# A one-core transformer block: a separate place for one running sum, and the next batch's tokens and keys prepared earlier

## What is computed

```python
def _tc_rmsnorm(x, t, gw, gb, bw, bb):
    g = (t @ gw.T + gb)[:, None, :]
    b = (t @ bw.T + bb)[:, None, :]
    return g * x * rsqrt(mean(x * x, -1) + EPS) + b

x1 = x + attention(_tc_rmsnorm(x, t, g1w, g1b, b1w, b1b), Wq, Wk, Wv, Wo)
y  = x1 + swiglu(_tc_rmsnorm(x1, t, g2w, g2b, b2w, b2b), gate_w, hid_w, out_w)
return x + y
```

## Time and profile before

| | before |
|---|---|
| median of 3 runs | 2479.52 us |
| lowest, highest | 2472.38, 2492.58 us |
| the profiled execution, device time | 2483.76 us |
| its span, first to last instruction | 2481.9 us |
| PE busy | 2309.7 us (93%) |
| DVE busy | 1676.2 us (68%) |
| POOL busy | 1454.4 us (59%) |
| ACT busy | 1310.9 us (53%) |
| mean granted TensorE clock | 0.976 |

### The profile page before, as it was taken

How to read it: one execution, slowest core, us unless ns; L and a number is a source line. 1 busy time by engine, 2 the same in 40 slices (tenths; PEclk the granted TensorE clock), 3 DMA queues, 4 the chain that set the end, 5 groups by cost and what they waited for, 6 DMA issues and landing times. The chain is left out here.

```text
span 2481.9 us, 40287 instructions
## 1 busy us (share of the span) xinstructions
PE 2309.7 (93%) x10884; PEld 1572.9 (63%) x10884; DVE 1676.2 (68%) x2732; ACT 1310.9 (53%) x2319; POOL 1454.4 (59%) x1351
## 2 busy tenths in 40 slices
PE   5999989999989999989999848999999999999999
PEld 4655436554447555456554336888888888888887
DVE  4776734667725776537777347887788778778877
ACT  3366762566752667734667724445444534454454
POOL 0388981689970888944889925731572166216711
PEclk8999999999989999999999978999999999999999
DMA  5212203212122122132222043115412541254125
GB/s 179 81 41 63 64 14 108 52 41 67 48 71 64 38 69 52 47 95 52 51 57 60 21 162 136 60 60 179 151 54 69 170 154 52 74 164 157 47 81 174
DMA packets 92656, 209.60 MB, mean 84 GB/s; under 512 B 15632, under 2 KB 15632, under 8 KB 90640
## 3 DMA queue, kind: packets, MB, share of 16 engines
q1 hardware_dynamic: 91344, 202.71, 27.2%
q0 software_dynamic: 1088, 4.19, 0.4%
HBM read 134.23 MB, written 19.92 MB: 62 GB/s over the span
## 5 line engine op out<-in xcount | busy, mean ns | idle before, releaser
L680 DVE TENSOR_REDUCE pmax<-bank 128x1 f32<-128x512 f32 x1024 | 653.7, 684 | 197.0 <-PE bank L893 187.6
L599 ACT ACTIVATE probs<-bank 128x512 f32<-128x512 f32 x1024 | 572.0, 600 | 330.6 <-PE bank L973 249.5
L447 POOL TENSOR_TENSOR sums<-sums,probs 128x512 f32<-128x512 f32 x512 | 641.4, 1291 | 0.5 <-ACT probs L599 0.5
L447 POOL TENSOR_TENSOR sums<-probs 128x512 f32<-128x512 f32 x256 | 320.4, 1282 | 380.6 <-ACT probs L599 258.9
L973 PE MATMUL bank<-qs,ks 128*128 128x512 f32 x1024 | 441.3, 439 | 40.0 <-ACT probs L599 37.9
L893 PE MATMUL bank<-ks,qs 96*128 96x512 f32 x1024 | 402.9, 406 | 25.8 <-DVE pmax L680 25.1
L973 PEld LDWEIGHTS bank<-qs,ks 128*128 128x128 f32 x1024 | 192.8, 191 | 323.4 <-ACT probs L599 167.3
L1536 PE MATMUL bank<-H_hi,wt_hi 128*128 128x512 f32 x896 | 350.0, 391 | 14.6 <-DVE H_lo L1391 14.6
L1550 PE MATMUL bank<-ow,aw 128*128 128x512 f32 x1536 | 358.7, 392 | 0.0
L1536 PE MATMUL bank<-H_lo,wt_hi 128*128 128x512 f32 x896 | 349.6, 390 | 0.0
L1536 PE MATMUL bank<-H_hi,wt_lo 128*128 128x512 f32 x896 | 349.5, 390 | 0.0
(11 more groups left out here) (139 smaller groups left out, 3233.8 us busy)
## 6 DMA issues: line engine op xcount, KB each, us to landing
raw<-in_gu_w SPq DMA_DIRECT2D x66, 512.0 KB, 3.6
wo_raw<-in_out_w SPq DMA_DIRECT2D x128, 256.0 KB, 2.6
ks<-qk_hi SPq DMA_DIRECT2D x136, 128.0 KB, 2.4
qs<-qk_hi SPq DMA_DIRECT2D x264, 64.0 KB, 2.0
x<-in_x SPq DMA_DIRECT2D x10, 1024.0 KB, 5.2
ks<-qk_lo SPq DMA_DIRECT2D x68, 128.0 KB, 2.4
qs<-qk_lo SPq DMA_DIRECT2D x132, 64.0 KB, 2.0
wv<-wv_parts SPq DMA_DIRECT2D x4, 2048.0 KB, 8.9
```

What stands on the lines that cost most here:

```text
L447: nc.gpsimd.tensor_tensor(sums[:, h, :], first, probs[:, s % 2, h, :], ALU.add) \
L599: nc.scalar.activation(probs[:, s % 2, h, :], sbank[i % SB][:], ACT.Exp, scale=SCALE).then_inc(st_done, 1)
L680: nc.vector.reduce_max(pmax[:, t, h, hf:hf + 1], mbank[n % MB][:], AX_X).then_inc(sq_done, 1)
```

## The change

- The sum of head 0 in quad 0 goes into `yout[:, 0, :]`, a tile that the units do not otherwise use, and D of quad 0 reads it from there. POOL's wait for PE's reading of the previous quad moves from head 0 to head 1, in both quads. In unit 0 POOL waits instead for the store from `yout`.
- ACT's squares for the next batch no longer write their unused output to `yout` but to a half of `qk_hi`, after the copies of an earlier K have been stacked.
- Tokens of the next batch: half 0 is loaded in unit 1 instead of 3. Squares move from (u, s) = (4, 4) to (3, 4) and from (6, 3) to (5, 5), mean squares from (4, 5) and (6, 5) to (3, 5) and (5, 7), inverse roots on POOL from (4, 5) and (6, 6) to (3, 6) and (6, 0), scaling from (4, 6) and (6, 7) to (4, 1) and (6, 2).
- DVE's waits for the next batch's gain and bias move from (5, 0) to (4, 2), and so does ACT's.
- Transposed tokens: half 0 from unit 5 (cells 9, 13, 17, 24) to unit 4 (cells 15, 18, 24) and unit 5 (cell 8); half 1 from unit 7 (cells 13, 16, 19, 23) to unit 6 (cells 14, 17, 24) and unit 7 (cell 0). `load_x` of half 1 waits for the last tile of half 0, as before.
- The Q projections of the even units take four cells in a row instead of every second one. ("K", 8, 1) moves from cells 26 to 29 of unit 7 to cells 13 to 16.

```diff
-PROJECTED = {("K", 2, 1): (0, 1), ("Q", 2): (9, 2)}
+PROJECTED = {("K", 2, 1): (0, 1), ("Q", 2): (9, 1)}
 for odd in (1, 3):
     PROJECTED.update({("Q", odd + 2): (odd * UNIT, 1), ("K", odd + 3, 0): (odd * UNIT + 14, 1),
-                      ("K", odd + 3, 1): ((odd + 1) * UNIT, 1), ("Q", odd + 3): ((odd + 1) * UNIT + 9, 2)})
-PROJECTED.update({("Q", NU - 1): (5 * UNIT, 1), ("Q", NU): (6 * UNIT + 8, 2), ("K", NU, 0): (7 * UNIT + 8, 1),
-                  ("K", NU, 1): (7 * UNIT + 26, 1)})
-HT_AT = {5: (9, 13, 17, 24), 7: (13, 16, 19, 23)}
+                      ("K", odd + 3, 1): ((odd + 1) * UNIT, 1), ("Q", odd + 3): ((odd + 1) * UNIT + 9, 1)})
+PROJECTED.update({("Q", NU - 1): (5 * UNIT, 1), ("Q", NU): (6 * UNIT + 8, 1), ("K", NU, 0): (7 * UNIT + 8, 1),
+                  ("K", NU, 1): (7 * UNIT + 13, 1)})
+HT_AT = {(4, 15): (0, 0), (4, 18): (1, 0), (4, 24): (2, 0), (5, 8): (3, 0),
+         (6, 14): (0, 1), (6, 17): (1, 1), (6, 24): (2, 1), (7, 0): (3, 1)}
...
+    def sum_place(quad, h):
+        return yout[:, 0, :] if (quad, h) == (0, 0) else sums[:, h, :]
...
-                    if u == 3:
+                    if u == 1:
                         load_x(b, 0, prepared)
...
-                        if (u, s) == (4, 5):
+                        if (u, s) == (3, 6):
                             inverse_root(b, b * 2 + 2)
-                        if (u, s) == (6, 6):
+                        if (u, s) == (6, 0):
                             inverse_root(b, b * 2 + 3)
...
                             pool.wait_ge(st_done, SCORES_T(b, NT + n * GH + h + 1) + SB)
-                            if s % QT == 1 and h == 0:
+                            if (u, s, h) == (0, 1, 0):
+                                pool.wait_ge(y_stored[0], b * (NT // 2 * 16) + 16)
+                            if s % QT == 1 and h == 1:
                                 pool.wait_ge(w_ready, MISC(b, sums_before(u, s // QT)))
...
-                            first = probs[:, 0, h, :] if s % QT == 1 else sums[:, h, :]
-                            nc.gpsimd.tensor_tensor(sums[:, h, :], first, probs[:, s % 2, h, :], ALU.add) \
+                            total = sum_place(s // QT, h)
+                            first = probs[:, 0, h, :] if s % QT == 1 else total
+                            nc.gpsimd.tensor_tensor(total, first, probs[:, s % 2, h, :], ALU.add) \
...
-                    if b is not None and hf == 0:
-                        for s in y_stored:
-                            act.wait_ge(s, b * (NT // 2 * 16) + 16)
+                    if b is not None:
+                        for s in k_stacked:
+                            act.wait_ge(s, b * (NG * HEAD_INC) + (3 + hf) * HEAD_INC)
...
-                nc.scalar.activation(yout[:, 0, :], x_tokens(b, hf)[:, t, :], ACT.Square,
+                unused = yout[:, 0, :] if b is None else qk[0][:, 1, :].bitcast(F32)
+                nc.scalar.activation(unused, x_tokens(b, hf)[:, t, :], ACT.Square,
...
-                            if (u, s) == (4, 4):
+                            if (u, s) == (3, 4):
                                 square(b, 0, h)
-                            if (u, s) == (4, 6):
+                            if (u, s) == (4, 1):
                                 scale_x(b, 0, h)
-                            if (u, s) == (6, 3):
+                            if (u, s) == (5, 5):
                                 square(b, 1, h)
-                            if (u, s) == (6, 7):
+                            if (u, s) == (6, 2):
                                 scale_x(b, 1, h)
...
-                        if (u, s) == (4, 5):
+                        if (u, s) == (3, 5):
                             mean_square(b, 0)
-                        if (u, s) == (6, 5):
+                        if (u, s) == (5, 7):
                             mean_square(b, 1)
...
-                    last = nc.tensor.matmul(wbank[DH * h:DH * h + DH, :], ones[:], sums[:, h, :], start=True, stop=True)
+                    last = nc.tensor.matmul(wbank[DH * h:DH * h + DH, :], ones[:], sum_place(quad, h), start=True, stop=True)
```

More of the change, by code:

```diff
@@ L105, in made_at @@
     q = s * GH + h
-    if u in HT_AT and q in HT_AT[u]:
-        return ("hT", HT_AT[u].index(q), list(HT_AT).index(u))
+    if (u, q) in HT_AT:
+        return ("hT", *HT_AT[u, q])
     return ("mT", u + 1) if (s, h) == MAXIMA_AT and u < NU - 1 else None
@@ L585, in _ @@
                         act.wait_ge(pv_done, b * (NU * NS) + n + 1)
-                        if u == 5 and s == 0:
+                        if u == 4 and s == 2:
                             act.wait_ge(const_dve, b * 2 + 4)
@@ L779, in _ @@
                                                     ALU.max).then_inc(const_dve, 1)
-                        if (u, s) == (4, 5):
+                        if (u, s) == (3, 5):
                             mean_square(b, 0)
-                        if (u, s) == (6, 5):
+                        if (u, s) == (5, 7):
                             mean_square(b, 1)
-                        if (u, s) == (5, 0):
+                        if (u, s) == (4, 2):
                             dve.wait_ge(const_dve, b * 2 + 4)
```

## The result

| | before | after |
|---|---|---|
| median, us | 2479.98 (5 runs) | 2501.84 (5 runs) |
| lowest, highest | 2472.38, 2492.58 | 2499.19, 2504.41 |
| span of the profiled execution | 2481.9 | 2502.6 |
| DVE busy | 1676.2 | 1757.1 |

The ratio of after to before is 1.009, with a 95% interval of 1.0071 to 1.0108. The forecast was 2444 us, its range 2425 to 2472: wrong in size and in sign.

The account below looks back on a forecast made before the run. POOL's loop was taken to bound plain units, 1.3 us above PE's, and POOL to set unit 7's end. Terms summed to −10.1 us per batch, put at −9.0, four times −36: 2444 us, range 2425 to 2472.

Parts of the forecast that it names:

- What bounds the kernel, and the place: Plain units: POOL's loop, 34.9 us, exceeds PE's 33.55; with the place PE sets the length, gaining 4.0 up to unit 4.
- The moved work: Token tiles moved between units 4 to 7: unit 4 +1.7 us, unit 6 +2.1, unit 5 −1.8 to 33.3.
- The Q projections: Four cells in a row make DVE wait for ACT's copy: 0.5 us each in units 0 and 2, bound 1.2.
- Unit 7 and the tail: POOL ends 37.7 us into unit 7; unit and tail take 59.0 us against 68.3, a gain of 9.3.
- The step that failed: Moved work in other units: claimed none conflicts on the shared port, as tokens' low parts read PSUM and one SBUF tile.
- the rule about the shared port: DVE operations with two SBUF inputs and GpSimd operations reading SBUF exclude each other; used for 0.9 us in unit 7.
- Half of it: Rival: DVE bounds units 4 and 6, 2.5 us more in each, −16 us in all: 2464; chance 0.18.
- Slower by the clock: Rival: idle time in units 5 and 7 holds the tail's matmuls at 1.2 GHz, +60 us, 2540; chance 0.08.

Follow-up runs that it names:

- experiment 1: The kernel before with only the place for head 0 and the squares' unused output in `qk_hi`; tokens, K and Q unmoved: 2440.79 us, ratio 0.9852.
- experiment 3: The kernel after with the next batch's mean squares on ACT instead of DVE, at (3, 5) and (5, 6): 2458.41 us, ratio 0.9913.
- experiment 4: The kernel of experiment 3, with POOL also waiting in unit 7 for DVE's first two low parts of the output: 2436.40 us, ratio 0.9826.
- experiment 9: The kernel of experiment 4 with the Q projections of units 0 and 2 at every second cell again: 2429.95 us, ratio 0.9791.
- experiment 6: The kernel after with POOL's inverse roots four additions earlier, at (3, 5) and (5, 7): 2467.74 us in one run.
- experiment 7: The kernel of experiment 4 with a needless DVE tensor_scalar of 128 x 4 in five places of each batch: 2473.85 us in one run.
- experiment 10: The kernel after with POOL's two pauses for the low parts of the output, mean squares still on DVE: 2490.13 us in one run.
- experiment 11: The kernel after with POOL's wait at head 0 again in the second quad only: 2456.0 us in one run.
- experiment 2: The kernel after without the place for head 0, so the moves alone; POOL waits for D at head 0 again: 2462.11 us, ratio 0.9929.
- experiment 5: The kernel after with both POOL waits back at head 0, the sum still in `yout`: 2465.55 us in one run.

## Why the prediction was wrong

**What bounds the kernel, and the place: right in kind.** POOL's loop was longer than PE's by 1.3 us, and without its wait PE sets the length. Units 1 and 3 take 32.98 us wherever nothing else disturbs them (experiments 1, 3, 4), with 0.1 us of PE idle. POOL's idle time at the first quad fell from 3.17 us to 1.96 + 0.57 in unit 1 and 1.27 + 0.57 in unit 2 of batch 3 (forecast near 2). Only the 0.57 of it is a wait for D; the rest waits for exponentials, since PE now sets the pace. At the second quad, where none was forecast, it is 0 in unit 1 but 0.92 + 0.61 in unit 2. The 33.6 us forecast for these units was the busy time of PE in unit 2, which holds for unit 2 (33.74 in experiment 9) and is 0.6 too much for units 1 and 3. The place alone gains 5.5 us a batch in units 0 to 3 (experiment 1), where the prediction had 4.0.

**The moved work: right in unit 4, by luck in unit 6.** Forecast +1.7 and +2.1 us, measured +1.2 and +2.05. The waits were the expected ones: 0.99 and 1.56 us for the tokens' low parts ahead of the maxima tile, 0.7 and 0.3 on row maxima. But unit 6's loss is the clock: with the mean squares on ACT it takes 32.84 us at 1.00, 0.5 less than before. The forecast number came by another mechanism than the one it was made of. Unit 5 was to fall to 33.3 us and took 39.90 with the stall; without it, at full clock, it takes 33.5 (experiment 9). The dip doesn't hang on unit 5's stall alone, though: in experiment 9, without that stall, unit 6 took 33.0 us at 1.00 in two batches and 35.4 at 0.90 in the other two.

**The Q projections: mis-sized.** I took 0.5 us each in units 0 and 2. They cost 35.86 − 34.25 = 1.6 and 34.93 − 33.74 = 1.2 us (experiments 4 and 9), beyond or at my upper bound of 1.2. In batch 1, at full clock in both, it is 1.4 and 1.0: 0.7 and 0.6 are waits on row maxima, the rest is in PE's busy time. The bound counted DVE's wait and the low part, not that DVE also makes the reciprocals there; that these are the difference is not shown.

**Unit 7 and the tail: half right.** POOL's last addition ended 36.4 us into the unit (forecast 37.7); 1.0 of the difference is that the last eight additions took 9.86 us and not 10.90, for here DVE stood still beside them. Forecast was a gain of 9.3 us; measured 5.5, with DVE's port free 8.2 (60.06 us). The missing 2.7 us are the first low part of the output, 9.17 us instead of about 1.

**The step that failed** is the sentence "Nothing that the change moves into other units is of that kind". The prediction had the rule about the shared port, and used it for 0.9 us in unit 7 alone. It listed the low parts of the tokens as harmless, which they are (0.69 us in the mean before and after), and did not name the mean square, a tensor_scalar from SBUF to SBUF, so that it stood at nothing without a reason. It cost 43 us. And it read the earlier trace rows as POOL being slowed by DVE, where the other direction, DVE stopped by POOL, was the dear one. The profile of before showed it: 1457 ns in the mean for a 167 ns instruction. It also took POOL's pauses for pure loss, where they were what let DVE in.

With that step mended, the rest of the sum holds, in part by luck. The kernel of experiment 4 is the change without the port's losses: its units 0 to 3 gained 2.7 us a batch over before (forecast 2.8), units 4 to 6 lost 0.6 net (forecast 2.0), unit 7 with its tail gained 8.2 (forecast 9.3). It took 2436.4 us, the forecast for the change was 2444. In units 0 to 3 two errors cancel: the place gave 1.5 us more than was forecast, and the Q projections cost 1.8 more. In units 4 to 6 it is unit 6 that came out 1.6 below its forecast. The price of DVE's stalls per batch, as after less its remedy: 4.95 in unit 3 and 5.57 in unit 5 (after less experiment 3), 2.55 in unit 6 by the clock (an upper value, as experiment 9 shows), 2.7 in the last unit and tail: 15.8, four times 63 us. 2501.8 − 63 = 2439.

**The rivals.** Half of it, by DVE as the bound in units 4 and 6: not seen. Slower by the clock: stretches at half clock are there, behind DVE's stalls in units 3, 5 and 7 of every batch, the longest of some 10 us, and some elsewhere (units 0, 2, 4 and 6), but none lasts through a tail. None of the rivals was the one that came; the change was slower by something that no rival named.

**What the moves are worth.** Attention ends at 1404.3 us in the profile of the place alone, and at 1403.8 in that of experiment 9, which has the place, the moves and three remedies. What units 4 to 6 lose by the moved tokens, unit 7 gains. Of the 11 us between their medians little is in attention's own matmuls: behind these points the two profiles have 1032.0 and 1026.9 us. From PE's first feed-forward product on both take 1004.0. The 5 us lie ahead of it (27.9 and 23.0 us without a matmul), where DVE's copy of the last output tile starts 7.4 us behind PE's last product in the one, after a wait of 5.0 us for a store from `yout`, and 2.4 us behind it in the other. The rest is spread of the runs: the profile of the place alone is its fastest run, that of experiment 9 nearly its slowest. So in attention the place, a few lines, is nearly the whole gain, and by the medians about three quarters.

## What to carry to other kernels

When a change takes the pauses out of GpSimd (POOL), list every VectorE (DVE) instruction that runs beside it and compare its mean time with its time alone; a tiny one that is many times too long in the profile of before is the warning (here 1457 ns against 167). If it must run there, put it on another engine or give GpSimd a wait on its result, at a place where GpSimd has time. Test the halves of a change alone, since two halves that each gain can lose together.

## What was not expected of the hardware

The Trainium skill (SBUF — State Buffer, Who interferes with whom) says that a tensor_scalar in its two-port mode contends with GpSimd for a shared port pair, and a VectorE instruction with two SBUF inputs with a GpSimd instruction that reads SBUF, that whoever issues first has the pair for the whole instruction, and that tensor_reduce on this chip never contends. The last agrees: 0.144 us in the mean over twenty. That it is a port is the Trainium skill's account; the runs show which instructions wait, and until when. "For the whole instruction" doesn't go far enough: a wait of one addition would be 1.25 us, and DVE waited through four whole additions in unit 3 (5.72 us), seven in unit 5 (9.29) and seven in unit 7 (9.17), until POOL stopped. POOL's own additions were not slowed: eight in 9.87 us, 1.23 each, where four in unit 2 of before took 5.03.

When DVE gets its turn, the moment between two back-to-back additions, stays open. With 12 to 18 POOL operations since a pause of 0.3 to 0.6 us it lost every turn in nearly all cases (after; experiments 3, 6, 7, 10; in batch 0 of experiment 7 it won the fifth, 5.14 us), and it lost one or none with 4 to 6 operations since a pause of 0.3 to 0.8 us (experiments 1, 7, 11), or with 18 or 19 since a pause of 1.3 to 3.3 us (experiments 2, 5). But the place alone won the first turn with 12 operations since a pause of 0.19 us, and experiment 10 lost four turns in three batches and one in the fourth, in the same place. So neither the count nor the pause alone is the rule, and what decides is not shown; small differences of time may.
